# A graph network on one NeuronCore: x is added to the fourth gate layer's sums two layers earlier, and eight weight slabs are staged at the hand-over

## The chip, the cores and the metric

One core of one Trainium2 chip. The metric is device time in microseconds of one execution, the median of the runs. Engines: PE is TensorE (PEld its weight loads), DVE is VectorE, ACT is ScalarE, POOL is GpSimd, SP is SyncE, which here only issues DMAs. Each engine works through its own instruction list in order; semaphores tie the lists together.

## The reference

Four graph blocks over 1250 nodes of 1024 features in fp32; each ends with a residual sum and a layer norm. The change lies in the first block and at its seam to the second:

```
x1 = x @ W1 + b1                       # 1250 x 512
g  = x1
for k in range(4):                     # four gate layers
    alpha = tanh(g_dst . gw_k[:512] + g_src . gw_k[512:] + gb_k)
    g = g + segment_sum(norm * alpha * g_src, dst)
h  = layernorm(x + concat([x1, g]))    # left half x + x1, right half x + g
...                                    # then two SAGE layers, GAT, GCN
```

## The kernel before

**Tiling.** The nodes form NT = 10 blocks of T = 125. A product is one job, an entry of JOBS; its number j orders the work of all engines. Jobs 0 to 9 are x1, 10 to 49 the four gate layers with ten jobs each, 50 to 59 the z products of the second block (x times the first half of the SAGE weights), and so on. Every engine's program is a loop over j; in iteration j it does what belongs to job j, and other steps for jobs nearby.

**A gate job** (`m_product`, lines 831 to 867) multiplies, for each of ten source blocks s, Mh with Zh, Mh with Zl and Ml with Zh: fp32 data split in a high and a low part, 30 matmuls of 512 columns. M is built ahead of that: ACT writes tanh into Tt (L989, ten instructions, three gates ahead), DVE multiplies Tt by the edge counts Ar (L1233), ACT casts it to Mh (L969, two gates ahead), DVE takes the rest as Ml (L1219). There are two Tt and three Mh and Ml. Afterwards DVE adds the product to G (L1342). In layers 0 to 2 it goes on with two reductions over G for the next layer's gates (L1267, L1270) and the low part of z (`z_lower`, L1258), ACT with the high part (L1004).

**Layer 3, before.** POOL adds for each gate x1 (loaded again from yl_d) and the left half of x into U (L1655), and the right half of x into G (L1658); this is `ahead`, called for j + 1 behind `soon(j - 1)`. SP loads three R tiles for it (L649 to L651, issued on L582; there are four R tiles). U has two buffers and is free when XO has been written from it. DVE's G (L1342) waits for the second addition (L1341), then come the statistics (`stats`, L1274). DVE seeds the inverse root one iteration later (`soon`), POOL refines it (`newton`, L1615 to L1621, 13 small instructions), ACT writes XO in iteration j + 2 (`apply`, L1045, L1046; two XO buffers, each free when its store has landed), TensorE transposes it (L909, eight instructions in `tail`, behind the product of j + 3), ACT copies XT (L1071) and issues both stores (L1081 xT_d, L1091 x_d).

**Weights.** A half of a weight matrix is eight slabs of 128 rows; slab g goes through a staging tile (`stage`, L564), ACT casts it to wh (`slab`, L943), DVE (even g) or POOL (odd g) takes the rest as wl (L1193, L1629). In layers 1 and 3, z lives in wh, wl and the two xl tiles (`ZB`): sources 0 to 7 are wh and wl 0 to 7, sources 8 and 9 the xl tiles. So the second block's weights (slabs 8 to 15) and its first two xl can be written only while the last gate job, 49, is using up its sources. It signals s_ms after each source.

**Order at the hand-over, before.** `staging(g)` gives six staging tiles in turn: ws0, ws1 and four halves of the Tt tiles. Slabs 14 and 15 share ws0 and ws1 with 8 and 9 and wait for their wl (`stage_free`). xl of job 50 waits for nine sources, xl of job 51 for the whole gate (L1201 to L1204). ACT casts six slabs, then does `apply(47)`, then the last two. POOL does `soon` and `ahead` in front of its slabs. In iteration LAST_GATE + 2, SP loads both GW tiles (512 KB each, L638).

In layers 0 to 2 POOL has no instruction, SP one Ar load per gate (L631; it waits until DVE's Tt of two gates before has read the tile).

```
for s in range(NT):
    ...
    te.matmul(o, Mh[i][:, s, :], zh, start=(s == 0), stop=False)
    ...
    if j == LAST_GATE and s < NT - 1:
        m.then_inc(s_ms, 1)
```

Of the kernel before, what the change touches and what calls it, by code (L numbers as in the profile page):

```python
# [8 lines left out]
T = 125  # L9
# [116 lines left out]


# [52 lines left out]
def staging(g):  # L180

    return (g - 8) % 6 if 8 <= g < 80 else g % 2
# [3 lines left out]
for _h in range(1, NH):  # L186
    _f, _slabs = LAST_X[_h - 1], list(range(8 * _h, 8 * _h + 8))
    _ring = 6 if 2 <= _h <= 9 else 2
    if _h == 1:
        STAGE_AT[LAST_GATE - 3], STAGE_AT[LAST_GATE - 1], STAGE_AT[LAST_GATE] = _slabs[:2], _slabs[2:6], _slabs[6:]  # L190
    elif FIRST_X[_h] - _f <= 5:
        STAGE_AT.setdefault(_f - 3, []).extend(_slabs[:_ring])
        SLAB_AT.setdefault(_f, []).extend(_slabs)
        STAGE_AT.setdefault(_f, []).extend(_slabs[_ring:])
    else:
        _s = max(_f + 1, 14)
        for _i in range(0, 8, 2):
            STAGE_AT.setdefault(_s + _i, []).extend(_slabs[_i:_i + 2])
            SLAB_AT.setdefault(_s + _i + 1, []).extend(_slabs[_i:_i + 2])
# [117 lines left out]
def gnn_program(nc, xT, x, es, ed, win, W1, b1, gw, gb, Ws0, Wn0, b0, Ws1, Wn1, bb1, W2, a2, W3, b3, out):  # L317
# [14 lines left out]
    yl_d = dram("yl_d", (NT, 128, HW), f32)  # L332
    m_d = dram("m_d", (NT, 128, NT * T), f32)
# [11 lines left out]
    with ctx:  # L345
# [79 lines left out]
        STG = [ws[0][:], ws[1][:]] + [TF[i // 2][:, (i % 2) * HW:(i % 2) * HW + HW] for i in range(4)]  # L425
# [3 lines left out]
        d_stage = [sem(f"d_stage{i}") for i in range(6)]  # L429
# [5 lines left out]
        d_yl = [sem(f"d_yl{i}") for i in range(2)]  # L435
        d_a = [sem(f"d_a{i}") for i in range(2)]
# [39 lines left out]
        def r_release(q, i):  # L476

            if i < 0:
                return
            j = R_BY[i]  # L480
            if j in W2_AT:
                q.wait_ge(s_w2, W2_AT[j] + 1)
            elif JOBS[j].kind == "gate":
                q.wait_ge(s_pu, 2 * JOBS[j].d + 2)
# [53 lines left out]
        def stage_free(q, g):  # L538

            if g < 2:  # L540
                return
            o = next((i for i in range(g - 1, -1, -1) if staging(i) == staging(g)), None)
            if o is not None:
                slab_split(q, o)
            elif staging(g) > 1:
                t_release(q, 38 + (staging(g) - 2) // 2)
# [11 lines left out]
        def sync_program(_):  # L558
# [73 lines left out]

            def late(j):
# [57 lines left out]
            for j in range(NT - 1, NJ):  # L691
# [5 lines left out]
                if j == LAST_GATE:  # L697
                    for g in STAGE_AT[j]:
                        stage(g)
# [3 lines left out]
                if j != LAST_GATE:  # L703
                    for g in STAGE_AT.get(j, []):
                        stage(g)
# [5 lines left out]
        def tensor_program(_):  # L711
# [119 lines left out]
            def m_product(j):  # L831
# [5 lines left out]
                for s in range(NT):  # L837
# [5 lines left out]
                    te.matmul(o, Mh[i][:, s, :], zh, start=(s == 0), stop=False)  # L843
                    if full:
                        te.matmul(o, Mh[i][:, s, :], zl, start=False, stop=False)  # L845
                        q.wait_ge(s_ml, part)
                        m = te.matmul(o, Ml[i][:, s, :], zh, start=False, stop=(s == NT - 1))  # L847
# [7 lines left out]
                    if j == LAST_GATE and s < NT - 1:  # L855
                        m.then_inc(s_ms, 1)
# [76 lines left out]
        def scalar_program(_):  # L933
            q = Waiter(ac)

            def slab(g):
                h = g // 8
                q.wait_ge(d_stage[staging(g)], 16 * stage_count(g))
                if h == 1:
                    q.wait_ge(s_ms, g % NSLOT + 1)  # L940
                elif h:
                    q.wait_ge(s_mm, LAST_X[h - 1] + 1)
# [81 lines left out]
            def apply(j):  # L1024
# [5 lines left out]
                if f == 0:  # L1030
                    left, right = U[i % 2], G[:, JOBS[j].d, :]
# [124 lines left out]
            for j in range(NT - 1, NJ + 3):  # L1156
# [5 lines left out]
                if j == LAST_GATE:  # L1162
                    for g in range(8, 14):
# [3 lines left out]
                if j == LAST_GATE:  # L1167
                    for g in range(14, 16):
                        slab(g)
# [14 lines left out]
        def vector_program(_):  # L1184
# [129 lines left out]
            def u_free(j):  # L1314

                prev = [o for o in PJ if o < j and (JOBS[o].kind in ("att", "kept", "loop") or JOBS[o].second
                                                    or (JOBS[o].kind == "gate" and JOBS[o].layer == 3))]
                for o in prev[-2:]:
                    if JOBS[o].layer == 1 and o != prev[-1]:
                        q.wait_ge(s_tt, GROUPS[o][-1][0] + 1)  # L1320
                    elif JOBS[o].layer == 1 and JOBS[j].layer != 1:
                        q.wait_ge(s_tt, GROUPS[o][-1][0] + 1)
                    if JOBS[o].kind == "gate" and (o != prev[-1] or JOBS[j].kind != "gate"):
                        q.wait_ge(s_xo, FI[o] + 1)
                    if JOBS[o].kind != "gate":
                        q.wait_ge(s_post, PI[o] + 1)

            def post(j):
# [8 lines left out]
                elif job.kind == "gate":  # L1337
                    k = job.layer
                    q.wait_ge(s_mm, j + 1)
                    if k == 3:  # L1340
                        q.wait_ge(s_pu, 2 * d + 2)  # L1341
# [9 lines left out]
                    else:  # L1351
                        stats(j, U[FI[j] % 2], G[:, d, :])
# [217 lines left out]
            for j in range(NT - 1, NJ + 3):  # L1570
                if j == J0[0] + 2:
                    large_known()
                if j == z0:
                    second(z1)
# [32 lines left out]
        def gpsimd_program(_):  # L1607
# [36 lines left out]
            def ahead(j):  # L1644

                job = JOBS[j]
                if not (job.kind == "gate" and job.layer == 3):
                    return
                d, u = job.d, U[job.d % 2]
                r0, r1, r2 = R_OF[j]  # L1650
                r_landed(q, r0)
                r_landed(q, r1)
                if d >= 2:
                    q.wait_ge(s_xo, d - 1)
                po.tensor_tensor(u, R[r1 % 4], R[r0 % 4], ALU.add).then_inc(s_pu, 1)  # L1655
                r_landed(q, r2)
                q.wait_ge(s_zl, 3 * NT + d + 1)
                po.tensor_tensor(G[:, d, :], R[r2 % 4], G[:, d, :], ALU.add).then_inc(s_pu, 1)  # L1658
# [50 lines left out]
            for j in range(NT - 1, NJ + 3):  # L1709
# [64 lines left out]
```

## Time and profile before

| | us |
|---|---|
| median of 3 runs (1735.94 to 1737.6) | 1737.48 |
| the profiled execution, its own time | 1738.19 |
| its span, first to last instruction | 1736.4 |
| DVE, ACT, POOL busy | 928.5, 720.9, 342.5 |
| mean granted TensorE clock | 0.964 |

The profiled execution took 0.7 us more than the median; its span is 1.8 us shorter than its time. In the table by stretches, 249.4 to 321.1 us is gate layer 1 as TensorE sees it (layer 2 follows until 392.8), 392.8 to 480.8 the other nine gates of layer 3 behind its first, 480.8 to 558.4 the ten z products. A busy time per engine is followed by the number of its instructions. PEclk is the granted clock as a share of full speed. In the order of time, "x10" is the number of instructions merged into a row, and the bracket says how long the engine had stood idle and what released it.

### The profile page before, as it was taken

Reading aid. Unit: us, or ns where it says so; the run is one execution under the profiler, and the core shown is the slowest. Engines: PE = TensorE matmul, PEld = TensorE weight load, DVE = VectorE, ACT = ScalarE, POOL = GpSimd, SP = SyncE. Lnnn points to the kernel's source line nnn. Section 1 sums busy time; section 2 is a strip of 40 time slices with the busy share of each in tenths; the row PEclk is TensorE's granted clock in tenths of the full one; section 3 lists DMA queues with packets and bytes.
Section 4 is the critical chain, followed back from the end, with each engine's and each line's share of the span. In section 5 each row is a group of like instructions: output and inputs, shape, how many; then the busy total and the mean of one; then the engine's idle time right before and its main releaser. Section 6 shows DMA issues by size and latency. Waiting matters only on the chain.

```text
span 1736.4 us, 19661 instructions
## 1 busy us (share of the span) xinstructions
PE 1579.8 (91%) x7072; PEld 1259.9 (73%) x7072; DVE 928.5 (53%) x1457; ACT 720.9 (42%) x1246; POOL 342.5 (20%) x670
## 2 busy tenths in 40 slices
PE   4797999998869999999999999996978899999995
PEld 3676788886657787788778777775756678787774
DVE  8686778775435434322442435555466637633345
ACT  4355767665533334333332233343322234543233
POOL 4132000006640001100110103122244204301015
PEclk9899999999989999999999999998988899999998
DMA  4223211114655543433453344444334235545335
GB/s 140 74 85 131 75 55 47 45 33 163 226 199 188 186 137 107 147 120 108 124 174 121 112 150 129 160 166 155 97 120 128 93 132 190 200 163 182 94 105 167
DMA packets 99002, 226.80 MB, mean 131 GB/s; under 512 B 22647, under 2 KB 25582, under 8 KB 98896
## 3 DMA queue, kind: packets, MB, share of 16 engines
q1 hardware_dynamic: 84486, 177.67, 32.3%
q10 hardware_dynamic: 14410, 47.74, 7.5%
q8 instruction: 64, 1.05, 0.3%
q14 instruction: 42, 0.34, 0.1%
HBM read 168.62 MB, written 56.75 MB: 130 GB/s over the span
## 4 chain that ended last, share of the span: by engine, by line
PE 64%; DVE 15%; POOL 7%; ACT 6%; issue 4%; DMA 4%; ACTq 0%; DVEq 0%; SPq 0%; POOLq 0%
PE bank L727 12%; PE bank L729 12%; PE bank L728 12%; PE bank L843 10%; PE bank L854 6%; PE bank L847 4%; PE bank L845 4%; DMA x_d<-XO 2%; PE bank L778 1%; PE bank L909 1%; ACT Mh L969 1%; DVE Ml L1219 1%; ACT XO L1046 1%; DVE oK L1503 1%; DVE st L1280 1%
## 5 line engine op out<-in xcount | busy, mean ns | idle before, releaser
L727 PE MATMUL bank<-wh,xh 128*125 128x512 f32 x1040 | 424.7, 408 | 28.9 <-issue 13.5
L728 PE MATMUL bank<-wl,xh 128*125 128x512 f32 x1040 | 413.7, 398 | 0.0
L729 PE MATMUL bank<-wh,xl 128*125 128x512 f32 x1040 | 413.2, 397 | 0.0
L843 PE MATMUL bank<-Zh,Mh 125*125 125x512 f32 x1000 | 405.2, 405 | 8.4 <-ACT Mh L978 3.5
L1205 DVE TENSOR_TENSOR xl<-xs,xh 128x1000 fp32r<-128x1000 f32 x120 | 146.7, 1225 | 298.9 <-ACT xh L952 298.9
L952 ACT CAST xh<-xs 128x1000 fp32r<-128x1000 f32 x130 | 133.0, 1025 | 301.1 <-PE bank L729 285.2
L727 PEld LDWEIGHTS bank<-wh,xh 128*125 128x125 f32 x1040 | 195.3, 188 | 77.9 <-issue 28.4
L854 PE MATMUL bank<-Zl,Mh 125*125 125x512 f32 x600 | 237.5, 396 | 0.0
L729 PEld LDWEIGHTS bank<-wh,xl 128*125 128x125 f32 x1040 | 195.6, 188 | 50.3
L843 PEld LDWEIGHTS bank<-Zh,Mh 125*125 125x125 f32 x1000 | 189.2, 189 | 55.6 <-issue 6.3
L728 PEld LDWEIGHTS bank<-wl,xh 128*125 128x125 f32 x1040 | 196.0, 189 | 44.8
L847 PE MATMUL bank<-Zh,Ml 125*125 125x512 f32 x400 | 162.2, 405 | 0.0
L845 PE MATMUL bank<-Zl,Mh 125*125 125x512 f32 x400 | 162.2, 405 | 0.0
L854 PEld LDWEIGHTS bank<-Zl,Mh 125*125 125x125 f32 x600 | 111.9, 187 | 27.2
L989 ACT ACTIVATE Tt<-PB,Q 125x125 f32<-125x125 f32 x400 | 120.5, 387 | 3.6 <-ACT XT L1071 3.6
L1629 POOL TENSOR_TENSOR wl<-Tt,wh 128x512 fp32r<-128x512 f32 x24 | 35.0, 1469 | 356.4 <-ACT wh L943 356.4
L969 ACT CAST Mh<-Tt 125x1250 fp32r<-125x1250 f32 x56 | 69.3, 1238 | 84.3 <-DVE Tt L1233 62.8
L969 ACT CAST Mh<-Ar 125x1250 fp32r<-125x1250 int16 x60 | 74.2, 1237 | 66.6 <-DVE Ar L1249 52.1
L1629 POOL TENSOR_TENSOR wl<-ws,wh 128x512 fp32r<-128x512 f32 x32 | 47.9, 1502 | 259.0 <-ACT wh L943 259.0
L1362 DVE SCALAR_TENSOR_TENSOR U<-bank,DEGI,B 125x512 f32<-125x512 f32 x40 | 29.9, 747 | 120.8 <-PE bank L854 120.8
L847 PEld LDWEIGHTS bank<-Zh,Ml 125*125 125x125 f32 x400 | 76.8, 192 | 19.8 <-DVE Ml L1224 0.2
L1219 DVE TENSOR_TENSOR Ml<-Tt,Mh 125x1250 fp32r<-125x1250 f32 x56 | 81.5, 1455 | 17.5 <-ACT Mh L969 17.5
(162 smaller groups left out, 2062.3 us busy)
## 6 DMA issues: line engine op xcount, KB each, us to landing
xs<-xT_d SPq DMA_DIRECT2D x80, 500.0 KB, 3.6
Ar<-a_d SPq DMA_DIRECT2D x100, 312.5 KB, 3.4
xs<-hT_d SPq DMA_DIRECT2D x40, 500.0 KB, 3.6
x_d<-XO ACTq DMA_DIRECT2D x30, 512.0 KB, 3.8
R<-x_d SPq DMA_DIRECT2D x60, 256.0 KB, 4.1
xT_d<-XT ACTq DMA_DIRECT2D x30, 500.0 KB, 2.7
ws<-in_W SPq DMA_DIRECT2D x34, 256.0 KB, 3.4
m_d<-Tt ACTq DMA_DIRECT2D x10, 625.0 KB, 4.6
```

What stands on the lines that cost most here:

```text
L727: te.matmul(o, xh[i % 2][:, k, :], wh[s][:], start=(k == 0), stop=False)
L728: te.matmul(o, xh[i % 2][:, k, :], wl[s][:], start=False, stop=False)
L729: m = te.matmul(o, xl[i % 2][:, k, :], wh[s][:], start=False, stop=(k == 7))
L843: te.matmul(o, Mh[i][:, s, :], zh, start=(s == 0), stop=False)
L845: te.matmul(o, Mh[i][:, s, :], zl, start=False, stop=False)
L847: m = te.matmul(o, Ml[i][:, s, :], zh, start=False, stop=(s == NT - 1))
L854: m = te.matmul(o, Mh[i][:, s, :], zl, start=False, stop=(s == NT - 1))
L952: ac.copy(xh[i % 2][:], xs[i % 2][:]).then_inc(s_xh, 1)
L969: ac.copy(Mh[i % 3][:], src[:]).then_inc(s_mh, 1)
L989: m = ac.activation(t[:, s, :], PB[:, d, :], ACT.Tanh, bias=PQ[k % 2][1][:, s:s + 1])
L1205: ve.tensor_tensor(xl[i % 2][:], xs[i % 2][:], xh[i % 2][:].bitcast(f32), ALU.subtract).then_inc(s_xl, 1)
L1219: ve.tensor_tensor(Ml[i % 3][:], M[:], Mh[i % 3][:].bitcast(f32), ALU.subtract).then_inc(s_ml, 1)
```

## The change

Four parts: (1) the additions of x move from layer 3 to layers 1 and 2. `ahead`, now called for j itself, adds the left sum in layer 1 into U, which SP stores to a new DRAM tensor ul_d, and x's right half into G in layer 2, behind z_lower. Layer 3 loads the left sum into R, and `stats` and `apply` read it there. R tiles per gate are 0, 2, 1, 1 by layer in place of 0, 0, 0, 3. (2) U's two tiles become staging tiles 6 and 7, so slabs 8 to 15 have eight; they are staged in iterations 45 (two), 46 (two) and 48 (four). (3) Gate job 49 takes its sources in the order 8, 9, 0 to 7, and xl of jobs 50 and 51 waits for the first and second of them. (4) At j = LAST_GATE each of ACT, DVE and POOL takes all its slabs together, before `apply(47)`, `post(49)` and `soon(48)`.

```diff
+LAST_ORDER = (8, 9) + tuple(range(8))
...
 def staging(g):
-    return (g - 8) % 6 if 8 <= g < 80 else g % 2
+    if 8 <= g < 16:
+        return (0, 1, 6, 7, 2, 3, 4, 5)[g - 8]
+    return (g - 16) % 6 if 16 <= g < 80 else g % 2
...
-        STAGE_AT[LAST_GATE - 3], STAGE_AT[LAST_GATE - 1], STAGE_AT[LAST_GATE] = _slabs[:2], _slabs[2:6], _slabs[6:]
+        STAGE_AT[LAST_GATE - 4], STAGE_AT[LAST_GATE - 3], STAGE_AT[LAST_GATE - 1] = _slabs[:2], _slabs[2:4], _slabs[4:]
...
-        many = 3 if job.kind == "gate" and job.layer == 3 else \
+        many = (0, 2, 1, 1)[job.layer] if job.kind == "gate" else \
...
+            def store_left(d):
+                q.wait_ge(s_pu, d + 1)
+                q.wait_ge(d_ul[d % 2], 16 * (d // 2))
+                sy.dma_start(ul_d[d], UF[d % 2][:]).then_inc(d_ul[d % 2], 16)
...
-                if job.kind == "gate" and job.layer == 3:
+                if job.kind == "gate" and job.layer == 1:
                     q.wait_ge(d_yl[d % 2], 16 * 5)
                     load_r(R_OF[j][0], yl_d[d])
                     load_r(R_OF[j][1], x[d * T:d * T + 128, 0:HW])
-                    load_r(R_OF[j][2], x[d * T:d * T + 128, HW:D])
+                    if d:
+                        store_left(d - 1)
+                elif job.kind == "gate" and job.layer == 2:
+                    if d == 0:
+                        store_left(NT - 1)
+                    load_r(R_OF[j][0], x[d * T:d * T + 128, HW:D])
+                elif job.kind == "gate" and job.layer == 3:
+                    q.wait_ge(d_ul[d % 2], 16 * (d // 2 + 1))
+                    load_r(R_OF[j][0], ul_d[d])
...
-                for s in range(NT):
+                order = LAST_ORDER if j == LAST_GATE else range(NT)
+                for n, s in enumerate(order):
...
-                if h == 1:
-                    q.wait_ge(s_ms, g % NSLOT + 1)
+                if h == 1 and g % NSLOT < NSLOT - 1:
+                    q.wait_ge(s_ms, LAST_ORDER.index(g % NSLOT) + 1)
...
                 if f == 0:
-                    left, right = U[i % 2], G[:, JOBS[j].d, :]
+                    left, right = R[R_OF[j][0] % 4], G[:, JOBS[j].d, :]
...
                 if j == LAST_GATE:
-                    for g in range(8, 14):
+                    for g in range(8, 16):
                         slab(g)
                 if j - 2 < NJ:
                     apply(j - 2)
-                if j == LAST_GATE:
-                    for g in range(14, 16):
-                        slab(g)
...
-                    if i == NT:
-                        q.wait_ge(s_ms, NT - 1)
-                    if i == NT + 1:
-                        q.wait_ge(s_mm, LAST_GATE + 1)
+                    if NT <= i < NT + 2:
+                        q.wait_ge(s_ms, LAST_ORDER.index(8 + i % 2) + 1)
...
                     if k == 3:
-                        q.wait_ge(s_pu, 2 * d + 2)
+                        q.wait_ge(s_pu, NT + d + 1)
...
                 if j == LAST_GATE:
+                    second(z0)
                     for g in range(8, 16):
                         if not on_pool(g):
                             slab(g)
-                    second(z0)
+                    second(z1)
...
             def ahead(j):
...
+                d = job.d
+                r = R_OF[j]
+                r_landed(q, r[0])
+                if job.layer == 1:
+                    r_landed(q, r[1])
+                    if d >= 2:
+                        q.wait_ge(d_ul[d % 2], 16 * (d // 2))
+                    po.tensor_tensor(UF[d % 2][:], RF[r[0] % 4][:], RF[r[1] % 4][:], ALU.add).then_inc(s_pu, 1)
+                else:
+                    q.wait_ge(s_zl, 3 * NT + d + 1)
+                    q.wait_ge(s_post, PI[j] + 1)
+                    po.tensor_tensor(G[:, d, :], R[r[0] % 4], G[:, d, :], ALU.add).then_inc(s_pu, 1)
...
-                if j - 1 < NJ:
-                    soon(j - 1)
-                if j + 1 < NJ:
-                    ahead(j + 1)
                 if j == LAST_GATE:
                     for g in range(8, 16):
                         if on_pool(g):
                             slab(g)
+                if j - 1 < NJ:
+                    soon(j - 1)
+                if j < NJ:
+                    ahead(j)
```

## Rows read from the trace of the kernel before

**Rows 1.** The page of the profile, part 1: busy us (share of the span), instructions.

```profile
PE 1579.8 (91%) x7072; PEld 1259.9 (73%) x7072; DVE 928.5 (53%) x1457; ACT 720.9 (42%) x1246; POOL 342.5 (20%) x670
```

**Rows 2.** Table by stretches: us; then busy us per engine, PEclk, DMA share, GB/s.

```profile
249.40:321.10 71.70, 71.70 (x322) 57.68 (x321) 56.36 (x83) 50.69 (x133) 0.00 (x0) 1.00 0.18 53
...
392.80:480.80 88.00, 73.60 (x325) 57.06 (x324) 45.58 (x75) 51.63 (x117) 59.54 (x116) 0.96 0.58 198
480.80:558.40 77.60, 63.27 (x275) 49.68 (x274) 31.95 (x55) 26.33 (x40) 17.66 (x39) 0.91 0.57 199
490.10:503.00 12.90, 8.73 (x25) 6.43 (x26) 3.35 (x6) 1.57 (x3) 8.43 (x16) 0.59 0.47 142
558.40:1736.40 1178.00, 1098.03 (x4792) 875.28 (x4790) 547.20 (x790) 407.26 (x531) 213.56 (x464) 0.97 0.43 139
428.00:438.00 10.00, 7.30 (x26) 5.56 (x25) 4.59 (x9) 5.82 (x13) 6.74 (x13) 0.83 0.54 184
```

**Rows 3.** List of waits, 392.8 to 558.4 us: total us, times, longest.

```profile
DVE G L1342 <- POOL G L1658: 24.3, 6, 5.3
...
POOL U L1655 <- ACT XO L1046: 18.9, 8, 2.5
```

**Rows 4.** Order of time, layer 3: start us, us, instruction, [idle before <- releaser].

```profile
443.18 1.25 ACT L969 CAST Mh<-Tt 125x1250 fp32r<-125x1250 f32 x1 [3.31 <-DVE Tt L1233]
...
445.74 1.02 ACT L1071 COPY XT<-bank 128x500 f32<-128x500 f32 x2
...
446.01 1.29 POOL L1655 TENSOR_TENSOR U<-R 125x512 f32<-125x512 f32 x1 [2.51 <-ACT XO L1046]
...
446.80 0.33 ACTq L1081 DMA_DIRECT2D xT_d<-XT  x1
...
447.66 3.01 ACT L989 ACTIVATE Tt<-PB,Q 125x125 f32<-125x125 f32 x10 [0.89 <-ACT XT L1071]
...
448.40 1.02 PE L909 MATMUL bank<-ident,XO 125*128 125x125 f32 x8
...
448.66 0.75 DVE L1342 SCALAR_TENSOR_TENSOR G<-bank,DD,G 125x512 f32<-125x512 f32 x1 [5.32 <-PE bank L847]
...
459.47 0.75 DVE L1342 SCALAR_TENSOR_TENSOR G<-bank,DD,G 125x512 f32<-125x512 f32 x1 [5.32 <-POOL G L1658]
```

**Rows 5.** Order of time, DVE behind the boundary to layer 1.

```profile
250.39 1.46 DVE L1233 TENSOR_TENSOR Tt<-Tt,Ar 125x1250 f32<-125x1250 f32 x1 [1.77 <-ACT Tt L989]
...
257.06 1.46 DVE L1233 TENSOR_TENSOR Tt<-Tt,Ar 125x1250 f32<-125x1250 f32 x1 [1.04 <-ACT Tt L989]
```

**Rows 6.** Order of time, POOL and DVE at 401 us, first gates of layer 3.

```profile
400.76 2.09 POOL L1655 TENSOR_TENSOR U<-R 125x512 f32<-125x512 f32 x1 [3.02 <-DMA R<-in_x]
...
401.62 2.54 DVE L1233 TENSOR_TENSOR Tt<-Tt,Ar 125x1250 f32<-125x1250 f32 x1
```

**Rows 7.** Order of time, the hand-over, by engine; the DMA row is the chain's.

```profile
482.72 13.37 SPq L564 DMA_DIRECT2D ws<-in_Wn  x2
...
480.19 2.17 ACT L943 CAST wh<-Tt 128x512 fp32r<-128x512 f32 x4
...
530.53 1.03 ACT L952 CAST xh<-xs 128x1000 fp32r<-128x1000 f32 x1 [3.68 <-PE bank L729]
...
536.10 1.03 ACT L952 CAST xh<-xs 128x1000 fp32r<-128x1000 f32 x1 [4.06 <-PE bank L729]
...
501.28 7.27 DMA x_d<-XO
...
490.13 0.76 PE L727 MATMUL bank<-wh,xh 128*125 128x512 f32 x1 [8.28 <-DVE xl L1205]
...
495.88 0.76 PE L727 MATMUL bank<-wh,xh 128*125 128x512 f32 x1 [4.13 <-POOL wl L1629]
```

**Rows 8.** DMA issues in layer 3 with KB and median landing; landing of R's loads.

```profile
x_d<-XO ACTq DMA_DIRECT2D x5, 512.0 KB, 3.8
...
DMA to landing us min/median/max: 2.8/4.1/6.4
```

More of the change, by code:

```diff
@@ L332, in gnn_program @@
     yl_d = dram("yl_d", (NT, 128, HW), f32)
+    ul_d = dram("ul_d", (NT, 128, HW), f32)
     m_d = dram("m_d", (NT, 128, NT * T), f32)
@@ L424, in gnn_program @@
         ZB = [(wh[n][0:T, :], wl[n][0:T, :]) for n in range(NSLOT)] + [(t[0:T, 0:HW], t[0:T, HW:2 * HW]) for t in XL]
-        STG = [ws[0][:], ws[1][:]] + [TF[i // 2][:, (i % 2) * HW:(i % 2) * HW + HW] for i in range(4)]
+        STG = [ws[0][:], ws[1][:]] + [TF[i // 2][:, (i % 2) * HW:(i % 2) * HW + HW] for i in range(4)] + [u[:] for u in UF]
         d_edge, d_gb, d_b = sem("d_edge"), sem("d_gb"), sem("d_b")
-        d_stage = [sem(f"d_stage{i}") for i in range(6)]
+        d_stage = [sem(f"d_stage{i}") for i in range(8)]
         d_xs = [sem(f"d_xs{i}") for i in range(2)]
@@ L435, in gnn_program @@
         d_yl = [sem(f"d_yl{i}") for i in range(2)]
+        d_ul = [sem(f"d_ul{i}") for i in range(2)]
         d_a = [sem(f"d_a{i}") for i in range(2)]
@@ L482, in r_release @@
                 q.wait_ge(s_w2, W2_AT[j] + 1)
-            elif JOBS[j].kind == "gate":
-                q.wait_ge(s_pu, 2 * JOBS[j].d + 2)
+            elif JOBS[j].kind == "gate" and JOBS[j].layer < 3:
+                q.wait_ge(s_pu, NT * (JOBS[j].layer - 1) + JOBS[j].d + 1)
             elif finishes(j) is not None:
@@ L544, in stage_free @@
                 slab_split(q, o)
+            elif staging(g) > 5:
+                q.wait_ge(d_ul[staging(g) - 6], 16 * (NT // 2))
             elif staging(g) > 1:
@@ L702, in sync_program @@
                         load(i)
-                if j != LAST_GATE:
-                    for g in STAGE_AT.get(j, []):
-                        stage(g)
+                for g in STAGE_AT.get(j, []):
+                    stage(g)
             for i in range(2):
@@ L842, in m_product @@
                     q.wait_ge(s_zl, z + s + 1)
-                    te.matmul(o, Mh[i][:, s, :], zh, start=(s == 0), stop=False)
+                    te.matmul(o, Mh[i][:, s, :], zh, start=(n == 0), stop=False)
                     if full:
@@ L846, in m_product @@
                         q.wait_ge(s_ml, part)
-                        m = te.matmul(o, Ml[i][:, s, :], zh, start=False, stop=(s == NT - 1))
+                        m = te.matmul(o, Ml[i][:, s, :], zh, start=False, stop=(n == NT - 1))
                     else:
@@ L854, in m_product @@
                         m = te.matmul(o, Mh[i][:, s, :], zl, start=False, stop=(s == NT - 1))
-                    if j == LAST_GATE and s < NT - 1:
+                    if j == LAST_GATE and n < NT - 1:
                         m.then_inc(s_ms, 1)
@@ L1314, in u_free @@
             def u_free(j):
-                prev = [o for o in PJ if o < j and (JOBS[o].kind in ("att", "kept", "loop") or JOBS[o].second
-                                                    or (JOBS[o].kind == "gate" and JOBS[o].layer == 3))]
+                prev = [o for o in PJ if o < j and (JOBS[o].kind in ("att", "kept", "loop") or JOBS[o].second)]
+                if len(prev) < 2:
+                    for g in range(8, 16):
+                        if staging(g) > 5:
+                            slab_split(q, g)
                 for o in prev[-2:]:
-                    if JOBS[o].layer == 1 and o != prev[-1]:
+                    if JOBS[o].layer == 1 and (o != prev[-1] or JOBS[j].layer != 1):
                         q.wait_ge(s_tt, GROUPS[o][-1][0] + 1)
[L1321 to L1326, printed above, removed]
+                    q.wait_ge(s_post, PI[o] + 1)
             def post(j):
@@ L1351, in post @@
                     else:
-                        stats(j, U[FI[j] % 2], G[:, d, :])
+                        r = R_OF[j][0]
+                        r_landed(q, r)
+                        stats(j, R[r % 4], G[:, d, :])
                 elif job.kind in ("mean", "self"):
@@ L1646, in ahead @@
                 job = JOBS[j]
-                if not (job.kind == "gate" and job.layer == 3):
+                if job.kind != "gate" or job.layer not in (1, 2):
                     return
[L1649 to L1658, printed above, removed]
+                d = job.d
[10 more added lines that the diff above has]
+                    po.tensor_tensor(G[:, d, :], R[r[0] % 4], G[:, d, :], ALU.add).then_inc(s_pu, 1)
             def second(j):
```

7 lines of the change are left out of this document (1 added, 6 removed).

## The prediction

> **What bounds the kernel now.** I began with the page's busy shares: TensorE is busy for 91% of the span [rows 1]. So only the places where it is not gapless can give anything. The table by stretches [rows 2] shows them. In gate layer 1 (249.4 to 321.1 us) TensorE is busy for all 71.70 us of its ten gates, at clock 1.00: 7.17 us a gate (layer 2 repeats it). In layer 3 (392.8 to 480.8) it is busy for 73.60 of 88.00. In the hand-over and the first ten z products (480.8 to 558.4) it is busy for 63.27 of 77.60, and the clock falls to 0.59 while the first of those products runs. Behind 558.4 it is busy again for 1098 of 1178 us, and the change leaves that work as it is.
>
> The list of waits over the two loose stretches names the holders [rows 3]: DVE waits 24.3 us for POOL's addition into G, POOL waits 18.9 us for ACT's XO. One gate of layer 3 in order of time [rows 4] shows the loop: ACT has written XO by 445.8, POOL adds U and then G, DVE may then start its G (448.66, after 5.32 us of idleness), the two statistics, Ml and Tt; Tt feeds ACT's Mh, which stands in front of the next XO. That DVE instruction comes again at 459.47: 10.8 us a gate, against 7.17.
>
> **Part 1: the two sums leave the fourth layer.** They are moved, not removed: yl and the left half of x are added during layer 1 (and stored to ul_d), the right half of x goes into G during layer 2, and layer 3 only loads ul_d. XO then waits for statistics and newton alone, and G for nothing of POOL's. What is late next? TensorE: a gate's 30 products (7.17 less the small row transposes) are about 7.04 us. The eight transposes of XO take about 1.0 more [rows 4], in front of the last gate for six gates. The first gate of the layer ends at 392.8, the start of that stretch [rows 2]; the other nine take 9 x 7.04 + 6 x 1.0 + 0.4 of row transposes = 69.8, so the last ends at 462.6. Second, the ACT loop, by its rows: Mh and XO 2.56 (443.18 to 445.74), XT 1.06, the two DMA issues 0.86, tanh 3.01, then Tt on DVE 1.4 and some 0.25 of hand-overs: 9.15 us. That is above TensorE's 8.05, but it holds for four gates only (the fourth to the seventh, as tanh is done three gates ahead). Behind a boundary the first Tt ends 2.4 us after the layer's first stretch begins (250.39 + 1.4 against 249.4, [rows 5]), here at 395.2. Two loops without XO and XT follow (6.0 each), one with XO (7.4), four in full (9.1 each): the last Tt ends at 451, and G, its statistics (2.4) and Ml (1.4) bring the last Ml to 454.8. TensorE wants it at 455.6, 7.0 before its end. So TensorE's own pace holds by less than a microsecond: the last gate ends at 462.7 in place of 480.8, **-18.1 us**. Bounds: no better than that. At worst the store of XO joins the loop: XO, XT and the issues (some 3.4 us of ACT) and the store's landing have to fit into one gate. In this layer a store lands in 3.8 us [rows 8]: 7.2, below 9.15; with the 7.27 seen at 501.28 [rows 7] it is 10.7, and 1.5 us more on four gates makes it -12.
>
> **Part 2: what layers 1 and 2 pay.** Added in layer 1, per gate: two 256 KB loads and one 256 KB store on SP's queue, one addition on POOL; in layer 2 one load and one addition. The DMA share there is 0.18 [rows 2], and SP only issues: about 0.43 us for one (ACT's two take 0.86, [rows 4]), 1.3 a gate at most. Its new wait (store_left for the previous gate's sum) has the next Ar load behind it; R lands 2.8 to 6.4 us after its issue [rows 8], the addition takes 1.3, so the sum is there about when SP would be waiting for Tt anyway. POOL has nothing else in these layers (0 instructions, [rows 2]). So DMA and SP are taken at nothing; if the cover failed, Ar would be late and Tt with it.
>
> The price is between POOL and DVE. The rows of 400 to 405 us [rows 6] show it: POOL's U needs 2.09 us where it takes 1.29 alone [rows 4], with its start under an Ml, and DVE's Tt, next in its queue, needs 2.54 in place of 1.46 [rows 5]. The two shut each other out, instruction by instruction. [...] So each of the 20 moved additions may hold DVE by 0 to 1.29 us. The slack: right behind a layer boundary DVE repeats every 6.67 us (Tt at 250.39, 257.06, with 1.04 us of waiting for tanh in front) [rows 5], 0.5 less than TensorE's 7.17, and this half microsecond is how it makes up its lateness. In layer 2 the addition waits for z_lower, so it meets Ml, comes in behind it, and takes 1.29 of a gap of 1.04: 0.25 us per gate, covered. In layer 1 it starts when R has landed, about 4.3 us behind Tt, and pushes the next Tt by 0.3 to 0.7: about the whole slack. DVE would then carry its 2 us of lateness to the next boundary, where the last two blocks of M and the next Ml have about 1 us in hand. I take 1 us per boundary, two boundaries: **+2 us**; bounds 0 and 8 (20 x 0.4, if every gate stood over the pace by that).
>
> **Part 3: the hand-over.** Before: the last gate ends at 480.84, the first z product starts at 490.13 after 8.28 us of waiting (xl), goes on at 495.88 after 4.13 more (wl) [rows 7], and runs at a clock of 0.59 [rows 2]. SP stood 13.37 us in the issue of the last two slabs, which share staging tiles with slabs 8 and 9 [rows 7]. The tenth product ends at 558.2: 77.3 us. After: eight staging tiles, the last four filled once Ml of the last two gates is done (454.8), landing in 3 to 6 us [rows 8], ahead of 462.7. With sources 8 and 9 first, xl is free after 0.7 and 1.4 us of the last gate, and the slabs after every further 0.7. Floor: ten products at 5.57 (xh at 530.53, 536.10) = 55.7, four transposes of XO at 1.0 = 4.0: 59.7, or 17.6 less than before. What remains on top: ACT is late by its loop (its XO of gate 46 ends near 460.4, xh of the second product near 463.3), so eight casts of 0.54 (four take 2.17 [rows 7]) end at 467.6, and the last wl on POOL at 469.5; about 0.7 us of wait. Then the stores of XO: that of gate 46 is issued near 471 together with the two 512 KB loads of GW, and before, the one beside them took 7.27 [rows 7]. XO of gate 48 would be ready near 480 and TensorE would want it at 477: 2.9; gate 49 another 1.5. Together 64.8, so **-12.5 us**. Bounds: -17.5 (stores at 3.8 us) and -7 (three stores at 7.3, with a slow clock behind the gaps).
>
> **Sum.** -18.1 + 2 - 12.5 = -28.6 us. The profiled execution took 1738.19 us, so 1709.6; the median of the runs is 0.7 lower, 1737.48, so **1709 us**.
>
> **Rivals.**
> (a) *The hand-over closes fully*: the stores take 3.8 us as in layer 3 and the locks cost nothing. -18.1 - 17.5 = -35.6: 1702. [...] Against: GW's loads still fall there. Chance 0.17.
> (b) *ACT and the stores pace layer 3, and boundaries cost more*: -12 + 5 - 10 = -17: 1720. For it: ACT's loop of 9.15 is above TensorE's pace and every further wait adds to it. Against: M is two gates ahead. Chance 0.20.
> (c) *The stall goes elsewhere*: the first mean jobs or the ul_d loads take back what was won, and the time stays within 3 us: 1737. Against: behind 558 TensorE is gapless and its loads follow its own pace. Chance 0.04.
> (d) *The lock makes it slower*: POOL's additions in layers 1 and 2 land in front of the gates' reductions and of Tt, and hold DVE 1.29 us in each of 20 gates. Then the cycle is 6.67 + 1.29 = 7.96, TensorE stops once a gate, and its clock goes with it: in 428 to 438 us, with one wait of 2.7 us, it was 0.83 [rows 2]. 20 x 0.8 = 16 us of waits and 143 us of work at 0.83, 29 us more: +45 - 28.6 - 2, about 1752. It decides from where the lock costs more than the 0.5 us of slack in most gates; to be slower than now waits and clock must take 30.6 us. Against: one gap of 1.04 us in front of Tt takes most of each addition, and the reductions start before R has landed. [...] Chance 0.05.
> The forecast has the remaining 0.54.
>
> **Numbers.** The forecast's own range is 1704 to 1716. The range for 8 in 10 reaches to (a) and to (b): 1701 to 1721. About 0.2% (3.5 us) is what a measurement of this kernel can tell from no change. Faster by more than that: the forecast, (a), (b), 0.91; within: (c), 0.04; slower: (d), 0.05.
>
> **What the profile after would show.** Right: no addition by POOL and no wait of DVE for POOL in layer 3; XO then waits for nothing but newton; the last gate ends 18 us earlier; SP's issue of slabs without a stand of 13 us; the first z product right behind the transposes, at full clock. Part 2 would show as Ml, Tt and POOL's addition of over 1.5 us in layers 1 and 2, with TensorE still gapless or with a wait near each boundary. Wrong: waits of TensorE for Ml or Mh inside layers 1 and 2 (d), a repeat of over 9.5 us in layer 3 (b), or new idleness of TensorE behind the z products (c).

## The result, and the profile after

The changed kernel takes 1710.74 us (median of 4 runs, 1708.83 to 1713.2) against 1737.54 before (4 runs): ratio 0.9847, 95% interval 0.983 to 0.9864, 26.8 us less. The forecast was 1709, from 1701 to 1721.

The page of the changed kernel: its span, and busy us (share of the span) by engine, beside [rows 1].

```profile
span 1707.0 us, 19694 instructions
...
PE 1574.6 (92%) x7072; PEld 1255.8 (74%) x7072; DVE 936.9 (55%) x1457; ACT 720.7 (42%) x1246; POOL 341.9 (20%) x670
```

The span is 29.4 us shorter than the one before (1736.4). Where these went is read off TensorE's order of time in both profiles, from the first instruction of each stage:

| stretch, us | before | after | |
|---|---|---|---|
| start of gate layer 1 | 242.2 | 238.7 | -3.5 |
| layer 1 | 71.75 | 72.16 | +0.4 |
| layer 2 | 71.71 | 71.71 | 0.0 |
| layer 3, first product to last | 95.19 | 79.66 | -15.5 |
| hand-over: from there to the end of the tenth z product | 77.32 | 62.16 | -15.2 |
| all behind it | 1178.2 | 1182.6 | +4.4 |

A stretch of products ends here where TensorE's pace would let the next instruction start. The change's own part is the middle: -15.5 - 15.2 + 0.4 = -30.3. The first line is no work of the change: in 60 to 100 us, the granted clock was 0.83 in the profile before and 0.91 in this one, and over the profiles of all kernels of this study layer 1 starts anywhere between 236.7 and 242.2 us. The last line holds code that the change leaves alone, and it varies as well (below). So a span tells two kernels apart to some 5 us only, and the stretches do it better.

The table by stretches of the changed kernel (us; busy us of PE, PEld, DVE, ACT, POOL; PEclk; DMA share; GB/s), the counterpart of [rows 2]:

```profile
238.70:310.90 72.20, 72.06 (x324) 57.72 (x322) 62.91 (x83) 50.46 (x131) 16.64 (x10) 1.00 0.48 158
310.90:382.60 71.70, 71.70 (x323) 57.72 (x322) 58.92 (x83) 50.58 (x131) 21.28 (x9) 1.00 0.27 86
382.60:462.20 79.60, 76.38 (x356) 60.76 (x356) 53.01 (x90) 56.35 (x128) 24.27 (x105) 1.00 0.53 178
462.20:524.40 62.20, 60.81 (x274) 47.30 (x273) 32.03 (x50) 27.15 (x41) 13.49 (x30) 1.00 0.66 231
524.40:1707.00 1182.60, 1101.95 (x4793) 877.14 (x4791) 547.13 (x790) 407.51 (x531) 214.00 (x464) 0.96 0.42 138
537.00:542.00 5.00, 4.95 (x15) 3.90 (x16) 1.06 (x1) 0.00 (x0) 0.00 (x0) 0.66 0.74 218
```

In layer 3 (382.6 to 462.2) TensorE has 76.38 us of work in 79.60 us, where it stood 14.4 of 88.0 before. In the hand-over it is busy for 60.81 of 62.20 at clock 1.00; the 0.59 of the first z product is gone. POOL's additions stand in layers 1 and 2, but the tenth of layer 2 falls behind layer 3's first product (9 are in the second row). The last row shows the next change of weights, where the clock falls to 0.66 behind a gap that the kernel before had too, there without the fall. That is 1.7 of the 4.4 us given back (5 us at 0.66 do the work of 3.3). It can't be put down to the change: of the eleven kernels of this study that have this gap (2.8 to 3.4 us), eight show the fall, also the one that takes over the hand-over part alone, and three don't (the one before and two that carry the change). The rest of the 4.4 is no more than this stretch varies by, 1178.2 to 1184.1 us in the kernels that leave it alone.

The list of waits, 382.6 to 524.4 us (us in total, times, longest), beside [rows 3]:

```profile
DVE st L1293 <- ACT XO L1064: 14.4, 7, 2.6
...
ACT XO L1063 <- DMA x_d<-XO: 4.1, 2, 2.2
...
PE bank L865 <- DVE Ml L1232: 3.2, 3, 1.1
...
PE bank L744 <- POOL wl L1641: 0.2, 1, 0.2
```

No wait for POOL's additions is left in the list, neither of DVE nor of XO. What took its place stands in the first row: DVE's statistics now wait for XO, 14.4 us in all, a wait that the prediction did not have. One gate of layer 3 shows it, ACT, then DVE, then TensorE (columns as in [rows 4]):

```profile
441.68 0.81 ACT L1063 ACTIVATE XO<-R,mv 125x512 f32<-125x512 f32 x1
...
445.02 3.01 ACT L1007 ACTIVATE Tt<-PB,Q 125x125 f32<-125x125 f32 x10 [0.89 <-ACT XT L1089]
...
440.55 0.75 DVE L1353 SCALAR_TENSOR_TENSOR G<-bank,DD,G 125x512 f32<-125x512 f32 x1
443.33 0.69 DVE L1293 BATCH_NORM_STATS2 st<-R 125x6 f32<-125x512 f32 x1 [2.02 <-ACT XO L1064]
...
444.97 1.45 DVE L1232 TENSOR_TENSOR Ml<-Tt,Mh 125x1250 fp32r<-125x1250 f32 x1
...
446.47 0.49 PE L865 MATMUL bank<-wh,Ml 125*125 125x512 f32 x1 [1.13 <-DVE Ml L1232]
...
455.62 0.50 PE L865 MATMUL bank<-xl,Ml 125*125 125x512 f32 x1 [1.06 <-DVE Ml L1232]
```

DVE is done with G at 441.3 but may start the statistics only at 443.33, when XO of gate i - 2 has been written: both use the same of two st and mv tiles. Ml, behind them, comes at 444.97, and TensorE stops for 1.13 us. So it goes for the last three gates, 9.15 to 9.22 us each, which is the ACT loop as priced.

### The profile page after: what moved, and what is told of

It is laid out like the page before. It is cut to its first block, busy times and chain, and to the rows that moved or that the text cites. A ratio compares the mean times of both kernels' runs of the same rounds, so it can differ in the third digit from the quotient of the medians.

```text
span 1707.0 us, 19694 instructions
## 1 busy us (share of the span) xinstructions
PE 1574.6 (92%) x7072; PEld 1255.8 (74%) x7072; DVE 936.9 (55%) x1457; ACT 720.7 (42%) x1246; POOL 341.9 (20%) x670
## 4 chain that ended last, share of the span: by engine, by line
PE 63%; DVE 16%; ACT 8%; POOL 5%; issue 5%; DMA 2%; ACTq 0%; DVEq 0%; SPq 0%; POOLq 0%
PE bank L744 12%; PE bank L746 12%; PE bank L745 12%; PE bank L861 10%; PE bank L872 6%; PE bank L865 4%; PE bank L863 4%; ACT Tt L1007 2%; DMA x_d<-XO 2%; ACT Mh L987 1%; PE bank L795 1%; DVE Tt L1246 1%; ACT XO L1064 1%; PE bank L927 1%; DVE Ml L1232 1%
## 5 line engine op out<-in xcount | busy, mean ns | idle before, releaser
L1627 POOL TENSOR_TENSOR mv<-mv 125x1 f32<-125x1 f32 x120 | 31.1, 259 | 323.5 <-DVE mv L1303 317.2
```

## The experiments

Each kernel was timed beside the kernel before, in 4 or 5 runs, the two with altered additions in 2. The stretches of their profiles, as in the table above; each is of one execution:

| | layer 1 | layer 3 | hand-over | behind | time, median | ratio to before, interval |
|---|---|---|---|---|---|---|
| before | 71.75 | 95.19 | 77.32 | 1178.2 | 1737.5 | |
| changed | 72.16 | 79.66 | 62.16 | 1182.6 | 1710.7 | 0.9847 (0.983 to 0.9864) |
| sums only | 73.73 | 80.40 | 68.18 | 1179.4 | 1714.8 | 0.9871 (0.9849 to 0.9893) |
| hand-over only | 71.75 | 95.18 | 68.98 | 1179.3 | 1729.5 | 0.9956 (0.9938 to 0.9974) |
| old order | 72.82 | 80.01 | 69.09 | 1181.3 | 1716.1 | 0.9876 (0.9852 to 0.99) |
| six tiles | 72.61 | 80.09 | 64.87 | 1180.4 | 1711.0 | 0.9849 (0.9827 to 0.987) |
| four st and mv | 72.37 | 81.2 | 66.4 | 1183.9 | 1715.1 | 0.9868 (0.9845 to 0.989) |
| additions twice | 75.79 | 81.70 | 61.99 | 1181.0 | 1713.5 | 0.9859 (0.9831 to 0.9888) |
| additions of 8 columns | 71.75 | 78.84 | 62.12 | 1184.1 | 1708.1 | 0.9829 (0.9799 to 0.9858) |
| second seam | 72.16 | 81.01 | 62.15 | 1177.2 | 1705.9 | 0.9821 (0.9796 to 0.9847) |
| store early | 72.49 | 79.97 | 60.75 | 1175.0 | 1701.4 | 0.9797 (0.9775 to 0.9819) |
| store early, four st and mv | 72.36 | 78.61 | 61.71 | 1178.7 | 1703.5 | 0.9798 (0.9775 to 0.9821) |
| these two and second seam | 72.71 | 78.52 | 61.46 | 1172.9 | 1698.0 | 0.9765 (0.9743 to 0.9786) |
| store early and second seam | 72.16 | 79.96 | 60.33 | 1170.2 | 1696.6 | 0.9772 (0.9757 to 0.9787) |

**The sums alone.** Staging, order of the sources and of the engines' steps as in the kernel before.

```diff
-LAST_ORDER = (8, 9) + tuple(range(8))
+LAST_ORDER = tuple(range(10))
...
-    if 8 <= g < 16:
-        return (0, 1, 6, 7, 2, 3, 4, 5)[g - 8]
-    return (g - 16) % 6 if 16 <= g < 80 else g % 2
+    return (g - 8) % 6 if 8 <= g < 80 else g % 2
```

> The changed kernel with only its first part: the sums with x are made in layers 1 and 2, but the hand-over is as before (six staging tiles, sources 0 to 9, old order on ACT, DVE and POOL). Theory (the two parts are worth what their stretches show, and add up): layer 3, from its first product to its last, 79.7 us as in the changed kernel, against 95.2 before; the stretch from there to the end of the tenth z product about 77, as before; time 1722 (1737.5 less 15.5). Rival (the faster layer leaves ACT late and the old hand-over takes it back): the hand-over stretch 82 or more, time 1727 or more. A further rival says that layer 3 gains only because of the new hand-over's order on POOL: then layer 3 stays above 85.

Layer 3 came out as expected (80.4), the time did not: 1714.8, 7 us less than the theory and 12 less than the rival. The missing part is in the hand-over, 68.2 in place of 77. The first product still waits for xl, as before the longest wait of the seam, but the second wait, 4.13 us for POOL's last wl [rows 7], is not there: without the two additions and XO's delay in front, POOL starts its first wl 3.9 us behind the last gate (469.66 against 465.78), where before it took 13.6 (494.48 against 480.84):

```profile
473.75 0.76 PE L746 MATMUL bank<-wh,xh 128*125 128x512 f32 x1 [6.95 <-DVE xl L1225]
```

**The hand-over alone.** Halves of GW, idle in layer 3, stand in for the U tiles.

```diff
+        UX = [GW[:, i, 0:HW] for i in range(2)]
...
-        STG = [ws[0][:], ws[1][:]] + [TF[i // 2][:, (i % 2) * HW:(i % 2) * HW + HW] for i in range(4)]
+        STG = [ws[0][:], ws[1][:]] + [TF[i // 2][:, (i % 2) * HW:(i % 2) * HW + HW] for i in range(4)] + UX
```

> The kernel before with only the hand-over part: eight staging tiles (the two more are halves of the idle GW tiles, as U is in use in layer 3), sources 8, 9, 0 to 7, slabs first on each engine. Theory: layer 3 stays at 95.2 us; the hand-over stretch falls from 77.3 to about 62, as in the changed kernel; time 1722. Rival (the hand-over can only be closed when POOL and ACT are free of layer 3's loop): the stretch stays above 70 and the time above 1729.

The stretch is 69.0 and the time 1729.5: nearly the rival, whose 70 the stretch just misses. All slabs are staged in time, yet TensorE waits 2.13 us for DVE's and 4.86 for POOL's wl, since these engines are still at layer 3's late gates:

```profile
481.05 0.76 PE L732 MATMUL bank<-wh,xh 128*125 128x512 f32 x1 [2.13 <-DVE wl L1196]
...
487.52 0.76 PE L732 MATMUL bank<-wh,xh 128*125 128x512 f32 x1 [4.86 <-POOL wl L1629]
```

So each part alone takes 8 to 9 us off the seam (9.1, 8.3), both 15.2. The seam was not the second part's alone, as the prediction had it.

**Order and tiles one by one.** The first of these runs also gives DVE its old order, xl of job 50 behind the four slabs.

```diff
-                if h == 1 and g % NSLOT < NSLOT - 1:
-                    q.wait_ge(s_ms, LAST_ORDER.index(g % NSLOT) + 1)
+                if h == 1:
+                    q.wait_ge(s_ms, g % NSLOT + 1)
...
-                    if NT <= i < NT + 2:
-                        q.wait_ge(s_ms, LAST_ORDER.index(8 + i % 2) + 1)
+                    if i == NT:
+                        q.wait_ge(s_ms, NT - 1)
```

> The changed kernel with the sources of the last gate in their old order 0 to 9 and the old waits of the first two xl (nine sources, and the whole gate), eight staging tiles kept. Theory: what the first z product waits for is the slabs' casts on a late ACT, so the order is worth little: TensorE waits 1 to 2 us for xl, hand-over stretch 64, time 1712.5. Rival (the order is what closes the gap): the wait for xl of 8.3 us comes back, stretch 70, time 1719.

> The changed kernel with six staging tiles for slabs 8 to 15 (slabs 14 and 15 share with 8 and 9 and are staged behind their split, ACT casts them behind XO as before), the new source order kept. Theory: slab 15 can only be staged when POOL has split slab 9, near the end of the last gate plus 2 us, lands 4 us later and is cast and split by plus 9; the first z product stands 3 to 5 us at its last part and the clock may drop; hand-over stretch 67 to 69, time 1716 to 1718. Rival (staging is hidden by the casts): stretch 62 to 63, time within 1 us of 1710.7.

For the order the rival was nearer: the wait of about 8 us and the stretch of 70 came, the time (1716.1) lies between 1712.5 and 1719. For the tiles the stretch (64.9) lies between the two, and the time (1711.0) is the rival's. With the old order the wait for xl is back at 7.09 us, although xs no longer waits for the slabs: on DVE, xl now stands behind four wl, which last from 464.01 to 469.7, beside POOL's own four, and itself takes 2.25 where others take 1.19. Which of the two, the sources' order or DVE's, brings it back was not tried. The stretch is 69.1, no better than with the old tiles (68.2):

```profile
472.03 0.76 PE L744 MATMUL bank<-wh,xh 128*125 128x512 f32 x1 [7.09 <-DVE xl L1220]
```

With the new order, six tiles cost 2.7 us of stretch (64.9), and the times of the two kernels can't be told apart. The eight tiles are worth something only behind the reordering, the reordering 7 us with them.

**The wait of the statistics.**

```diff
-        mv = [sb(f"mv{i}", [T, 6], f32) for i in range(2)]
+        mv = [sb(f"mv{i}", [T, 6], f32) for i in range(4)]
...
-                if i >= 2:
-                    q.wait_ge(s_xo, i - 1)
+                if i >= 4:
+                    q.wait_ge(s_xo, i - 3)
```

> The changed kernel with four tiles for the statistics (st and mv) in place of two, so that DVE's statistics of gate i no longer wait for XO of gate i - 2. Theory (what keeps layer 3 at 79.7 us instead of the forecast 77.0 is this wait of 1.95 us in front of Ml, which the forecast left out): TensorE's three waits of 1.0 to 1.1 us for Ml shrink to at most one below 0.5, layer 3 77.0 to 77.8, time 1708 to 1709. Rival (ACT's loop of 9.15 us alone sets the pace of the last gates): layer 3 stays at 79.5 or above and the gates still come every 9.15 us.

Both fell. TensorE's waits for Ml are gone, as the theory had it, and yet layer 3 is longer, 81.2, and the last gates come after 10.1 and 10.95 us, not 9.15. Behind a wait of 2.03 us for XT the clock is 0.68 as well (446.7 to 452.0). Waits and the chain of this run:

```profile
ACT XO L1063 <- DMA x_d<-XO: 8.0, 3, 5.2
...
PE bank L927 <- ACT XT L1089: 4.7, 3, 2.0
...
437.21 7.38 DMA x_d<-XO
...
447.58 7.95 DMA x_d<-XO
```

The store of XO lands 7.4 and 8.0 us after its issue, beside the loads of slabs and xs that fall into the same gates, and XO, XT and the transposes now wait for it. In the changed kernel the two stores of these gates took 6.0 to 6.2, only a little less:

```profile
L1109 ACTq DMA_DIRECT2D x_d<-XO x2: 389/389/389, 435.4 to 444.6; - x2
...
DMA to landing us min/median/max: 6.0/6.1/6.2
```

There the wait for XO on DVE was the one that showed; take it away and the next stands right behind.

**The lock.** POOL's additions twice, and cut to 8 columns:

```diff
+                    chain("p", po.tensor_tensor(XO[0][:, 0:HW], R[r[0] % 4], R[r[1] % 4], ALU.add))
+                    mine()
                     po.tensor_tensor(UF[d % 2][:], ...)
```

> The changed kernel with every addition of POOL in layers 1 and 2 made twice (the first into an XO tile that nobody reads then): 20 more instructions of 1.29 us, one behind the other. Theory (POOL and DVE shut each other out, and half a microsecond of slack per gate absorbs one addition but not two): in layer 1 Tt is held by up to 2.6 us in many gates, the stretch grows from 72.2 to 76 to 82 us; layer 2, where the second addition falls into G and the statistics' place, grows by 0 to 5. Rival (the lock is of no weight, POOL waits and DVE does not): both layers stay within 0.5 us of 72.2 and 71.7.

> The changed kernel with POOL's additions in layers 1 and 2 cut to 8 of 512 columns; the rest of x and x1 is left out of the sums, so the first block's output is another one. Theory (lock): Tt on DVE takes 1.46 us everywhere in layer 1 and the layer falls to 71.7 us, 0.4 to 2 us less than in the runs with full additions; layer 2 stays at 71.7. Rival (the longer layer 1 comes from SP's new waits or the DMAs, which are all still there): it stays at 72.2 or above.

Twice: layer 1 takes 75.8, just below the 76 to 82 that were expected; layer 2 doesn't move. With 8 columns layer 1 is back at 71.75, the value before the change, with every DMA and every wait of SP's still there. Tt of one gate in the run with double additions:

```profile
277.58 2.55 DVE L1246 TENSOR_TENSOR Tt<-Tt,Ar 125x1250 f32<-125x1250 f32 x1
```

and in the run with 8 columns:

```profile
273.88 1.46 DVE L1246 TENSOR_TENSOR Tt<-Tt,Ar 125x1250 f32<-125x1250 f32 x1 [1.05 <-ACT Tt L1007]
```

So what layer 1 pays is the lock: 0.4 us in the profile of the changed kernel, 0.4 to 2.0 over the runs that carry full additions, always 71.7 in layer 2.

Layer 3 pays too, though no addition belongs to it. Layer 2's last addition meets the two short Tt at the boundary, which take 1.83 us beside it; the kernel with 8 columns has them in 0.74 (POOL and DVE of the changed kernel, then DVE of that one):

```profile
385.65 1.35 POOL L1673 TENSOR_TENSOR G<-R,G 125x512 f32<-125x512 f32 x1 [5.04 <-DVE xl L1271]
385.44 1.83 DVE L1246 TENSOR_TENSOR Tt<-Tt,Ar 125x250 f32<-125x250 f32 x2
...
385.33 0.74 DVE L1246 TENSOR_TENSOR Tt<-Tt,Ar 125x250 f32<-125x250 f32 x2
```

It is 1.83 or 1.84 in every run with full additions. ACT's loop starts later by it and, being slower than TensorE, never makes it up: layer 3 takes 78.84 us with 8 columns, against 79.66 in the changed kernel and no less in any other with full additions and two st and mv tiles, and TensorE's waits for Ml fall from 3.2 to 2.4 us.

**The second seam.** Slabs 22 and 23 into the U tiles, all eight staged three jobs ahead.

```diff
+    if g in (22, 23):
+        return g - 16
```

> The changed kernel with the two U tiles as staging tiles 7 and 8 at the second seam as well (slabs 22 and 23, ahead of the first self product), where the trace of the changed kernel shows 3.2 us of waiting and then 3.4 us at half clock. Theory (slabs 22 and 23 are staged only when 16 and 17 are split, and ACT's xh stands behind their casts): the wait goes, the stretch behind the tenth z product is 3 to 5 us shorter, time 1706 to 1708. Rival (the wait is for xs, whose loads follow the same release): the wait stays at 2.5 us or more and the time within 1 us of 1710.7.

TensorE's order of time at this seam, the changed kernel:

```profile
537.05 0.47 PE L744 MATMUL bank<-wh,xh 128*125 128x512 f32 x1 [3.21 <-ACT xh L970]
```

and in this run, where what is left, 1.29 us, is no wait for xh:

```profile
534.51 0.47 PE L747 MATMUL bank<-wh,xh 128*125 128x512 f32 x1 [1.29 <-issue]
```

1705.9 against 1710.7: the theory (1706 to 1708, just missed downwards), though the two intervals overlap and the 5.4 us by which the stretch behind is shorter may be 1.0 (it was 1178.2 where it was shortest unchanged). Two more pairs stand further down.

**The store of XO one iteration earlier.**

```diff
                 tail(j - 3)
+                if 0 <= j - 2 < NJ:
+                    store_xo(j - 2)
```

> The changed kernel with ACT issuing the store of XO one iteration earlier (the store of gate i right behind XO of gate i, where it used to be that of gate i - 1), so that it has one gate more to land before its XO buffer is wanted. It does so in all blocks. Theory (in layer 3 three things stand one behind the other: DVE's wait of the statistics for XO, ACT's loop, and the stores, which land in 6 to 8 us beside the weight loads): this alone removes ACT's waits for the store (2.2 us in the changed kernel, 8.0 in the run with four tiles) but leaves the statistics' wait and ACT's 9.15 us, so layer 3 stays at 79 to 80 us, the hand-over at 61 to 62, time 1709 to 1711. Rival (the stores are what bounds the last gates): layer 3 falls to 77.5 or below.

> The early store of XO and four tiles for the statistics together. Theory (the four tiles alone lost because a quicker DVE only brought the stores into the loop): now neither is left, TensorE runs layer 3 at its own pace, 77.0 to 78.0 us with no wait for Ml and none for XT, hand-over 60 to 62, time 1707 to 1709. Rival (ACT's loop of 9.15 us bounds the last gates whatever else goes): layer 3 at 79.5 or above, time 1710 or more.

In layer 3 the first theory holds: 80.0 with the early store alone. The second holds in part: 78.6 with four tiles as well, 0.6 above its range, with no wait for Ml and, other than expected, 2.1 us for XT:

```profile
PE bank L927 <- ACT XT L1089: 2.1, 2, 1.0
```

Both times were missed: 1701.4, 9 us below the changed kernel, where 0 to 2 were expected, and 1703.5 where 1707 to 1709 were. The larger part, 7.6 us, lies behind the hand-over (1182.6 to 1175.0), and 5.3 of it in the last 280 us, in the last block, which ends in the same pair of XO buffers. Waits behind 1360 us in the changed kernel:

```profile
ACT XO L1063 <- DMA x_d<-XO: 20.2, 8, 5.4
```

and with the early store, where that row is no longer in the list and XO waits for newton alone:

```profile
ACT XO L1063 <- POOL mv L1702: 12.1, 6, 3.4
```

**Together.**

> Early store, four tiles for the statistics and eight staging tiles at the second seam together. Theory (the second seam is worth 4.8 us by its own run, and adds to the rest): 1702 to 1705, faster than the changed kernel and than each part alone. Rival (the early stores collide with loads in the later blocks, and what is won up to the hand-over is lost there): the rest behind the tenth z product is above 1181 us and the time is 1706 or more.

> Early store and eight staging tiles at the second seam, without the four tiles for the statistics. Theory (with the four tiles layer 3 is 1.4 us shorter and the hand-over 1 us longer by the profiles so far, so they are worth next to nothing): 1697 to 1700, not to be told from the run with all three; layer 3 at 79.5 to 80.5 us. Rival (the four tiles are a part of what made all three the fastest): 1701 or more.

1698.0, where 1702 to 1705 was expected, and 1696.6, just below 1697 to 1700: faster than either theory, which are still nearer than the rivals. The two can't be told apart, so the four tiles are worth nothing that shows. The second seam takes 4.8 us off the stretch behind beside the early store alone (1175.0 to 1170.2) and 5.8 with the four tiles too (1178.7 to 1172.9), so some 5 us in three pairs, and the medians differ by 4.8, 4.8 and 5.5. Not all of it is found at the seam: 1.9 to 3.3 us are gained within 370 us behind the hand-over, the other 2.7 to 3.0 lie 640 to 905 us behind it. That far stretch takes 257.2 to 257.8 us in one group of profiles and 260.1 to 260.7 in the other, and the faster group also holds the kernel before and four kernels without this edit; in the 20 us behind the last of its waits of 8.3 us the clock was 0.74 in the changed kernel (1323 to 1343 us) and 0.83 in the second seam's (1319.3 to 1339.3). Whether the edit has a part in that was not tried. Early store and second seam together beat both kernels: 0.9772 (0.9757 to 0.9787) of the kernel before, where the change alone gives 0.9847 (0.983 to 0.9864), 13 to 14 us more.

## Why the prediction was right, and where its terms were off

**The sum** said -28.6; the median fell by 26.8, the stretches of the change by 30.3. The terms missed by 1.6 to 2.7 us each, partly against one another, so that the total came out within 2 us is in part luck.

**Part 1, -18.1 forecast, -15.5 measured.** The step that failed is "G, its statistics (2.4) and Ml (1.4) bring the last Ml to 454.8 ... TensorE's own pace holds by less than a microsecond". Counted from the start of layer 3, the last Ml was done 3.8 us later than that (455.56 against 451.7), and with 0.8 us in hand this leaves 3.0 of the 3.2 us that TensorE waited. ACT's loop was priced right: 9.15 us, and the gates come at 9.15 to 9.22. But in front of the statistics stands `q.wait_ge(s_xo, i - 1)`, shown in the code and hidden in the trace of before behind POOL's additions. It holds the statistics, and Ml behind them, 1.95 to 2.02 us in each of the last gates that still have an Ml to come, and TensorE waited for the last three Ml. A second step had 1.2 us too little: "Behind a boundary the first Tt ends 2.4 us after the layer's first stretch begins" was read at the boundary to layer 1, where no addition ran; in layer 3 it ends 3.6 us after (393.33 against 389.77), held by layer 2's last addition, and 2.5 in the kernel with 8 columns. Some 0.6 us are spread over the rest. The bound of 77.0 was not reached in any run; the nearest, 78.5, needs four tiles and the early store. Rival (b) named the stores at 7.3 us as what would join the loop; they did (7.4 to 8.0) as soon as the statistics were let go.

**Part 2, +2 forecast, +0.4 measured in layers 1 and 2** (up to +2.0 in other runs). The mechanism was right. The two hold each other up, by 1.1 us where layer 2's addition starts under Ml (2.39 us, 1.30 alone), layer 2 absorbs it (71.71 us in both kernels), DMA and SP cost nothing (71.75 us for layer 1 in the run with 8 columns). "1 us per boundary, two boundaries" was near in sum and wrong in how it comes about at the second: layer 1 lost 0.4 us, layer 2 nothing, and at the boundary to layer 3 it was no lateness of DVE's but the last addition itself that held Tt, for 1.1 us. That cost layer 3 some 0.8, which stand above under Part 1; with them Part 2 cost 1.2. These rows of the changed kernel, POOL in layer 1, DVE, then POOL in layer 2, show the lock:

```profile
249.48 1.75 POOL L1669 TENSOR_TENSOR U<-R 128x512 f32<-128x512 f32 x1
255.55 1.30 POOL L1669 TENSOR_TENSOR U<-R 128x512 f32<-128x512 f32 x1 [4.32 <-DMA R<-in_x]
...
249.06 1.02 DVE L1280 CUSTOM_DVE_ANT_0 GSF<-G,GW 125x512 bf16<-125x512 f32 x1
...
250.12 1.66 DVE L1283 CUSTOM_DVE_ANT_0 GSF<-G,GW 125x512 bf16<-125x512 f32 x1
...
330.12 2.39 POOL L1673 TENSOR_TENSOR G<-R,G 125x512 f32<-125x512 f32 x1 [4.28 <-DVE wl L1271]
```

An addition alone takes 1.30 us; the one of layer 2 starts under Ml and takes 2.39. And the reductions, which take 0.69 alone, are held as well: 1.02 and 1.66 us around the addition of 249.48. The kernel before shows it too, ahead of the gate layers, where POOL takes the low part of x for the x1 jobs (DVE, then POOL):

```profile
92.94 2.60 DVE L1267 CUSTOM_DVE_ANT_0 GSF<-G,GW 125x512 bf16<-125x512 f32 x1
...
92.70 2.29 POOL L1687 TENSOR_TENSOR xl<-xs,xh 128x1000 fp32r<-128x1000 f32 x1 [13.65 <-ACT xh L952]
```

The longest of the 40 second reductions takes 1.66 us in the changed kernel (L1283), and 0.69 with 8 columns. Rival (d), which has the additions in front of the gates' reductions and of Tt, did not come: layer 2 kept its 71.71 us, since DVE had the slack (it still stands idle for 1.04 us in front of Tt at 325.73 and 332.40), and layers 1 and 3 lost 0.4 and 0.8.

**Part 3, -12.5 forecast, -15.2 measured.** Two steps of it failed. Stores beside GW's loads were taken at 7.3 us; XO of gates 48 and 49 came with 0.62 and 0.30 us of TensorE's waiting, not 2.9 and 1.5. The store of gate 46 was issued at 468.75, ahead of GW's loads at 470.8, and the stores from 460 to 491 us landed in 3.5 to 5.3 us; XO of gate 48 waited for newton (3.40 us), not for a store. And the gain was put down to tiles and order alone. The runs show that 9.1 us come with Part 1 alone.

**Rival (c)**, in which the stall goes elsewhere, did not come: behind the z products the same gap of 3 us as before comes with a fall of the clock, 1.7 us, but kernels with and without the change show such a fall or lack it.

## What to carry to other kernels

When a wait is taken out of a loop, list every wait in the code of the instructions behind it, not only those that the trace shows: two of them (the statistics' tiles, the store of XO) were invisible while POOL was late, and each cost time in turn. Price a lock between two engines at the boundaries too, where a slower engine's loop starts: 1.1 us there went straight into the next layer, while ten additions inside a layer cost 0 to 2. A two-buffer ring whose store is issued one iteration late has one iteration less to land; moving the issue was worth more here (1701.4 us against 1710.7) than two more tiles each for st and mv (1715.1). A reordering at a seam is worth its full amount only when the engines that carry it arrive in time: the hand-over fell to 62.2 us with the sums moved, and to 69.0 without.

## What the runs showed of the hardware beyond that

The granted clock of the same, unchanged stretch of 60 to 100 us lay between 0.83 and 0.92 over the profiles, and the start of layer 1 between 236.7 and 242.2 us; the latest starts came with 0.83, the earliest with 0.87, so that this clock isn't all of it. The fall to 0.66 behind the gap at 537 us appeared in the changed kernel and not in the one before, with gaps of 3.21 and 2.92 us; a gap of 2.76 us had it in the kernel with 8 columns and not in the one with the early store. What decides it was not tried.
